# Products of the identity as filler in further gaps of TensorE, in a post-norm decoder layer

## The reference

```python
# linear attention, 16 heads of depth 8
q = elu(x @ Wq + bq) + 1;  k = elu(x @ Wk + bk) + 1;  v = x @ Wv + bv
k = k / sqrt(sum(k * k, per head) + 1e-6)
y = x + (((q @ k.T) @ v) @ Wo + bo)            # per head, no softmax
x = layernorm(x + (layernorm(y) * gamma + beta))
# cross attention, 16 heads of depth 64, context of 64 rows per batch
x = layernorm(x + softmax(q2 @ k2.T / 8) @ v2 @ Wo2)
# feed-forward, operands rounded to FP4 in blocks of 16
h = silu(fp4(x) @ fp4(w_gate).T) * (fp4(x) @ fp4(w_up).T)
x = layernorm(x + fp4(h) @ fp4(w_down).T)
```

## Time and profile before

| | us |
|---|---|
| median of 3 runs | 360.56 (360.54 to 360.67) |
| the profiled execution's own time | 362.69 |
| its span, first to last instruction | 360.9 |
| TensorE busy | 342.2 (95%) |
| VectorE busy | 307.8 (85%) |
| GpSimd busy | 271.8 (75%) |
| ScalarE busy | 256.0 (71%) |
| mean granted TensorE clock | 0.994 of full |

### The profile page before, as it was taken

One profiled execution on the slowest core, in us unless ns is written; L12 is line 12 of the kernel. 1 busy time (PEld: TensorE's weight loads), 2 busy tenths in 40 slices (PEclk: granted clock), 3 DMA queues, 4 the chain that ended last, 5 costly groups with the idle time before them and its releaser, 6 DMA issues.

```text
span 360.9 us, 7621 instructions
## 1 busy us (share of the span) xinstructions
PE 342.2 (95%) x2319; PEld 288.1 (80%) x2319; DVE 307.8 (85%) x851; ACT 256.0 (71%) x533; POOL 271.8 (75%) x453
## 2 busy tenths in 40 slices
PE   6789999999999999999999999999999999989884
PEld 6588858787779979977799977888897888968763
DVE  1599986667799998988889988989999987999994
ACT  2678886776788685797857677877877767666543
POOL 3275779889978769798777578979979897794445
PEclk9899999999999999999999999999999999999999
DMA  7821100000100000111001000001000000001001
GB/s 233 290 62 31 39 8 16 0 16 2 46 29 2 1 2 0 45 32 31 0 2 40 7 1 17 15 3 29 2 1 17 1 16 15 4 15 31 0 23 37
DMA packets 13587, 10.46 MB, mean 29 GB/s; under 512 B 971, under 2 KB 12396, under 8 KB 13548
## 3 DMA queue, kind: packets, MB, share of 16 engines
q1 hardware_dynamic: 12540, 7.89, 7.2%
q10 hardware_dynamic: 1008, 2.10, 1.6%
HBM read 7.88 MB, written 2.10 MB: 28 GB/s over the span
## 4 chain that ended last, share of the span: by engine, by line
PE 52%; POOL 16%; issue 14%; DVE 11%; ACT 4%; DMA 1%; POOLq 0%; ACTq 0%; DVEq 0%
PE A L2880 11%; PE S L2850 8%; PE TP L2837 5%; PE TP L2868 5%; PE F L2904 4%; POOL pe L445 3%; PE A L2798 3%; PE A L2924 2%; PE S L2859 2%; POOL fold L439 2%; PE TP L2776 2%; POOL hv L455 2%; DVE smax L1838 2%; PE TP L2913 2%; DMA wqkT<-in_wk_t 1%
## 5 line engine op out<-in xcount | busy, mean ns | idle before, releaser
L445 POOL TENSOR_TENSOR pe<-pe,srec 128x1024 f32<-128x1024 f32 x32 | 60.8, 1905 | 5.0 <-DVE srec L1855 4.9
L2880 PEld LDWEIGHTS A<-wvoT,wqkT 128*128 128x128 f32 x480 | 56.1, 192 | 2.0 <-issue 1.2
L2880 PE MATMUL A<-wvoT,wqkT 128*128 128x128 f32 x480 | 57.3, 275 | 0.0
L2850 PE MATMUL S<-M,x1T 128*128 128x512 f32 x192 | 52.8, 410 | 0.7 <-DVE x1T L1737 0.7
L439 POOL TENSOR_TENSOR fold<-pe 128x512 f32<-128x512 f32 x32 | 42.1, 1314 | 12.6 <-ACT pe L1081 12.4
L2850 PEld LDWEIGHTS S<-M,x1T 128*128 128x128 f32 x192 | 34.0, 189 | 10.4 <-issue 1.8
L1838 DVE TENSOR_REDUCE smax<-S 128x16 fp32r<-128x1024 f32 x32 | 38.9, 1215 | 2.2 <-PE S L2850 2.2
L1086 ACT ACTIVATE wqkT<-TP 128x1024 f32<-128x1024 f32 x32 | 32.7, 1021 | 10.9 <-PE TP L2868 10.8
L1081 ACT ACTIVATE pe<-S 128x1024 f32<-128x1024 f32 x32 | 32.6, 1018 | 5.8 <-PE S L2859 5.6
L2868 PE MATMUL TP<-ident,pe 128*128 128x128 f32 x256 | 33.6, 274 | 0.5 <-ACT wqkT L1086 0.2
L2904 PE MATMUL F<-w_gu_r,xf_r 128*128 128x352 f32 x168 | 33.9, 337 | 0.1
(11 more groups left out here) (246 smaller groups left out, 914.6 us busy)
## 6 DMA issues: line engine op xcount, KB each, us to landing
xT<-in_x_t SPq DMA_DIRECT2D x16, 128.0 KB, 2.2
x_sb<-in_x SPq DMA_DIRECT2D x16, 128.0 KB, 2.2
out<-yf SPq DMA_DIRECT2D x15, 128.0 KB, 1.8
pe<-in_fw SPq DMA_DIRECT2D x1, 560.0 KB, 10.6
wqkT<-in_wq_t ACTq DMA_DIRECT2D x2, 256.0 KB, 4.8
wqkT<-in_wk_t ACTq DMA_DIRECT2D x2, 256.0 KB, 6.3
ctx_f<-in_ctx_t ACTq DMA_DIRECT2D x2, 256.0 KB, 7.4
wvoT<-in_wv_t ACTq DMA_DIRECT2D x1, 512.0 KB, 8.9
```

The source lines that it names most:

```text
L445: ge.tensor_tensor(w, w, spread(srec[n % NFO][:, :], HX, R), ALU.mult).then_inc(pn_made, 1)
L2850: last = te.matmul(S[:, half * BANK:half * BANK + BANK], part(x1T[b % 2][:, left, :], t), M[:, g % 2, right, HC * half:HC * half + HC, b % ...
L2880: last = te.matmul(part(A2, t), pT[n % 2][:, j, :], vo[b % 2][:, j, :], start=(j == 0 and b not in SUM_ON_PE), stop=(j == NJ - 1))
```

## The change

It adds fillers and nothing else: six products into bank S0 before `project_kv(1)`, three before `project_q(0)`, and in the last part 2 (TP0) before `h_transpose(11)`, one more (A2, 5 for 4) before `tile_xf_transpose(15, 0)`, 4 (S0) before `down(13)`, 2 (S0) before `tile_gate_up(15, 1)` and 2 (TP1) before `tile_h_transpose(15, 1)`. The waits added with them name counts that free the bank, or repeat the wait above them.

```diff
             project_kv(0)
             pe.wait_ge(fk_made, 1)
+            keep_warm(S0, 6)
             project_kv(1)
             g_product(1)
             pe.wait_ge(fk_made, 2)
+            keep_warm(S0, 3)
             project_q(0)
...
             pe.wait_ge(pT_kept, 30)
+            pe.wait_ge(pT_kept, 30)
+            keep_warm(TP0, 2)
             h_transpose(11)
...
             pe.wait_ge(hT_kept, 13)
+            pe.wait_ge(hT_kept, 13)
             keep_warm(TP0, 9)
             h_transpose(13)
             pe.wait_ge(yf_made, 13)
-            keep_warm(A2, 4)
+            pe.wait_ge(yf_made, 13)
+            keep_warm(A2, 5)
             tile_xf_transpose(15, 0)
             pe.wait_ge(xfT_kept, 16)
+            pe.wait_ge(hg4_made, 14)
+            keep_warm(S0, 4)
             down(13)
             pe.wait_ge(hg4_made, 15)
             tile_gate_up(15, 0)
             pe.wait_ge(yf_made, 14)
             tile_xf_transpose(15, 1)
             pe.wait_ge(hg4_made, 14)
+            pe.wait_ge(hg4_made, 14)
+            keep_warm(S0, 2)
             tile_gate_up(15, 1)
+            pe.wait_ge(hT_kept, 14)
             pe.wait_ge(hT_kept, 14)
             keep_warm(TP0, 7)
             h_transpose(14)
+            pe.wait_ge(xfT_kept, 17)
             pe.wait_ge(xfT_kept, 17)
             keep_warm(A2, 4)
             down(14)
             pe.wait_ge(hT_kept, 15)
             tile_h_transpose(15, 0)
             pe.wait_ge(hT_kept, 15)
+            pe.wait_ge(hT_kept, 15)
+            keep_warm(TP1, 2)
             tile_h_transpose(15, 1)
```

## The result

| | median, us | ratio to before (95% interval) |
|---|---|---|
| before | 360.68 (360.54 to 361.31) | |
| changed | 362.67 (362.16 to 363.08) | 1.005 (1.0039 to 1.006) |

The change made the kernel 2.0 us slower by the medians, 1.8 by the ratio (0.005 × 360.7). Forecast was +2.9, that is 363.5 us, with 363.0 to 364.0 as the forecast's own range and 361.7 to 364.4 over all rivals.

What follows compares the result with a forecast made beforehand. TensorE, busy 254.59 of 256.00 us from 60 to 316 us, was taken as the bound, VectorE after 346 us. Early fillers 2.2 plus last part 0.7 made 2.9: 360.56 + 2.9 = 363.5 us, range 361.7 to 364.4.

Steps and rivals of the forecast that it cites:

- First early filler: Six products before `project_kv(1)`, behind the wait: start 2.3 us later, kn(0) and `kv_outer(0)` about 2.05 us late.
- The half-clock price: First early filler: nine of its twelve records run at half clock, 0.22 us each.
- Rival 1: Early part: the clock doesn't fall, so the queues are only 0.5 us late, 361.8 us in all; 12%.
- Second early filler: Three products, 0.67 us, before `project_q(0)`: `kv_outer(0)` not hurt further, `q_negative(0)` 2.4 us late; both early fillers together 2.2.
- The last part: After 316 us: only the four products before `down(13)` cost, `tile_gate_up(15, 0)` starts 0.7 us late and that reaches the end.
- The slack of the other fillers: Last part: the fillers other than that before `down(13)` lie inside longer waits and cost nothing, one at most 0.05 us.
- the price of the waits: Added waits: on counts reached long before or repeating the wait above, so nothing, 0.05 us each at worst.
- the middle: From 60 to 316 us TensorE has some 1.4 us idle, all this part could take up; idle total forecast unchanged.
- rival 3: The filler before `down(13)` is hidden and the early one not: 362.8 us; 7%.
- rival 4: Not slower: fillers avert half-clock stretches of the timed runs' last part, 1.64 us each, 360.2 us with two; 4%.
- Rival 2: The early delay is swallowed before 60 us and only 0.7 stays: 361.3 us; 8%.

Runs made afterwards that it cites:

- e5: Kernel before plus only the six products before `project_kv(1)`, behind the wait for `fk_made` 1: 362.19 us, ratio 1.0029.
- e7: Kernel before plus the six products before `project_kv(1)`, placed ahead of the wait for `fk_made` 1: 360.97 us, ratio 0.9999.
- e9: Kernel before plus twelve products instead of six before `project_kv(1)`, behind the wait: 363.45 us, ratio 1.0068.
- e2: Kernel before plus both early fillers, six products before `project_kv(1)` and three before `project_q(0)`: 362.20 us, ratio 1.0040.
- e11: Kernel before without its own four `keep_warm` calls of the last part: 362.83 us, ratio 1.0052.
- e6: Kernel before plus only the three products before `project_q(0)`: 361.06 us, ratio 1.0003.
- e10: Kernel before plus all added fillers and waits of the last part except the four products before `down(13)` and their wait: 360.83 us, ratio 0.9995.
- e4: Kernel before plus only the four products before `down(13)`, with their added wait, behind the wait for `xfT_kept` 16: 361.49 us, ratio 1.0012.
- e12: The whole change, but with the six products and the four before `down(13)` ahead of their waits: 360.90 us, ratio 0.9995 to before.
- e8: Kernel before plus only the four products before `down(13)`, with their added wait, ahead of the wait for `xfT_kept` 16: 361.13 us, ratio 1.0000.
- e1: The kernel before, run once more with no edit: 360.95 us, ratio 0.9998.

## Why the prediction was right, and where it was not

**First early filler: the mechanism right, the size too large.** It stands behind the wait and pushes `project_kv(1)`, ScalarE's `k_exp(1)` and through it kn(0): e5 shows the push, e7 its absence when the filler stands ahead, e9 that it grows with the number. The term that failed is "I take 2.3, because the fall is in the rows". It assumed that "nothing before 11.74 is changed, so the clock falls as it did", but the clock doesn't fall at that place in every execution. Nine of the twelve records were costed at half clock, from one execution with a fall that no other profile shows there: in e2, e5 and in the changed kernel all twelve run at full clock and take 1.36 us, of which 1.15 to 1.19 go through. The text's own price for full clock, 1.34 us for the filler, was right within 0.02. The half-clock price, 0.22 us a record, was read from the opening filler, where the profile's granted clock stands at 1.00; the spacing there is twice the later one, and that is all that the rows show. A doubling at a granted 0.50 is in e11: 2.93 us for the twelve records of `down(13)` instead of 1.60.

**Rival 1 was right on the clock and wrong on the sum.** With the clock full it gave 0.5 us for the early part; measured 1.2. Its slip: it compared the end of `project_kv(1)` at full clock with the end that the half-clock execution had shown (14.01), and so booked as the filler's gain what belonged to the execution. The clock has to be the same on both sides of a difference. The two profiles side by side do show 0.45 (305.95 − 305.50), and would have seemed to bear it out.

**Second early filler.** "`kv_outer(0)` isn't hurt further" holds within 0.11 us (16.47 − 10.77 = 5.70 us after the wait, 5.59 in e5), and `q_negative(0)` is late (ScalarE waits 0.52 us for `project_q(0)` at 16.73). That this goes through, by 0.15 on the way from 2.05 to 2.2, fell: e6 is 0.0, taken up in the wait for kn(1). The claim that nothing ends idle time undelayed was too strong there.

**The last part.** `tile_gate_up(15, 0)` was forecast 0.7 us late and is (+0.67), in part by luck: the filler takes 0.99 us (341.97 to 342.96), not 0.89, and the slack behind `down(13)` is 0.32 (1.66 us from its start to `tile_gate_up` before, 1.34 now), not 0.2. The two slips cancel. The end moved 0.53 to 0.59 in the profiles and 0.36 to 0.43 timed: ScalarE's tanh comes 0.58 late, not 0.67, since the gate product itself is 0.1 shorter behind a dense run (1.35 against 1.45). The slack of the other fillers and the price of the waits, nothing, held (e10). So did the reading that the middle takes up next to nothing (0.06 us in e5).

**The chances.** The number on record nearest to 362.67 is rival 3's, 362.8. That is chance: it kept the early 2.2, which was 1.2, and left out the 0.7, which is there as 0.4 to 0.6. Rival 3, the filler before `down(13)` hidden, fell by e4; rival 4, a gain by averted half-clock stretches in the timed runs, fell by e12. Its premise was half right: over a third of the timed executions of before have a half-clock stretch, and with the three products before `project_q(0)` it is gone but once. But in the profiles it lies between 12 and 23 us, in none but e11's in the last part. And its price was too high: 1.64 us a stretch, where the one at 12 us cost 0.71 by the early distance and the later ones 0.1 or less. Rival 2, the early delay swallowed, is true of the three and not of the six.

**What stays open.** The price of the filler in an execution whose clock falls at 12 us wasn't measured; one of six executions of e2 took 363.56 us at a mean clock of 0.993, where the others lay from 361.86 to 362.48, which would fit it but isn't shown. Nor is it shown which filler holds the early clock: e5, with the six alone behind the wait, has no fall in 6 executions either. And where the stretch lay in the timed executions isn't recorded.

## What to carry to other kernels

A filler behind a wait is work on the path: it costs its length less the slack of whatever it pushes (1.15 of 1.36 us here, then all of 1.34 more). The same filler ahead of the wait was free in both places tried (e7, e8), where it is about as long as the wait or shorter and its bank is free by then. Before adding one, ask whether the clock falls at that place in more than one execution, and whether a later wait would pay for the fall anyway. A filler can do what it is for, hold the clock, and gain nothing.

Before sizing a term by one profile, set its own time beside the median of the runs: 2.1 us apart here said that the execution was untypical, and the terms that I built on its clock (2.05 for the first filler, rival 1's 0.5, rival 4's 1.64) were off. The mean clocks of the timed executions say how often a fall comes.

## What the runs showed of the hardware

The clock's fall isn't tied to a place in the program. The profile of before has it at 12.04 us, e7 near 15.6, e10 and e11 near 16.2, e9 near 19.5; e1 and the changed kernel have none early. In before and in e7 it fell after stretches with no idle spell over 1.34 us (before: 1.60 us of work in 4.00; e7: 2.03 in 3.50), so long idle spells aren't needed. What TensorE did doesn't decide it alone: from 12 to 15.5 us it was busy 2.27 us in e1 and 2.26 in e10, and only e10's clock fell behind that. And a half-clock stretch cost 0.71 us at 12 us and nothing that can be told at 15.6 or 16.2 us. The Trainium skill (TensorE: Matmul & The Clock Gate, "What's actually happening") calls the throttled state the default, released by activity; e11 agrees as far as it goes, with two falls in the last part once the filler is gone. The Trainium skill (same page, "Why this matters for your kernels") names only longer idle gaps as what drops the clock in the middle of a kernel; the rows here show falls with no idle spell over 1.34 us.

The landing of the bias rows, which lets the first projection start, moved from 5.99 us (e7) to 7.58 us (before) between profiled executions, by VectorE's first reading of them, and the first projection from 7.53 to 9.11. Two spans compared without an anchor behind that point tell nothing of a change of 1 us.
